# A two-layer decoder on one core: packed places on GpSimd, tiles' weights copied, four places and 2 KB pieces for the chosen experts

## What is computed

```
# layer 0: 32 experts (and two slices of a shared one), 4 per token, H = 128
scores = softmax(xf @ Wg); weights, indices = top_k(scores, 4)
for e in range(32):
    tok, w = tokens that chose e, their weights
    y = y.at[tok].add((silu(xf[tok] @ W1[e]) * (xf[tok] @ W3[e])) @ W2[e] * w)

# layer 1: 64 experts, 8 per token, 768 wide, at most 160 tokens for each expert
h = x_of_expert @ w1[e].T; x1, x2 = split(h)
out = (x1 * silu(x2)) @ w2[e].T          # weighted, and added to each token's row
```

## Time and profile before

| | us |
|---|---|
| median of 3 runs | 2603.03 (2599.43 to 2603.57) |
| the profiled execution | 2608.1 |
| its span | 2606.3 |
| packing rows | from about 383 to 580 |
| routed tiles | from 580 to 873 |
| chosen experts | from 1890 to 2606 |

### The profile page before, as it was taken

The page is one execution under the profiler, slowest core; times in us unless marked ns, Lnnn a source line. Parts: engine busy times, 40 slices in busy tenths (PEclk is TensorE's granted clock), DMA queues, the critical chain, the costliest instruction groups (busy, mean ns, idle before and its releaser), DMA issues. The chain is left out here.

```text
span 2606.3 us, 39064 instructions
## 1 busy us (share of the span) xinstructions
PE 2210.4 (85%) x11638; PEld 1487.9 (57%) x11639; DVE 1300.6 (50%) x2816; ACT 821.2 (32%) x1855; POOL 833.1 (32%) x1016
## 2 busy tenths in 40 slices
PE   6999759719999556888888887999999999999996
PEld 3445436507777322333343334656588888888885
DVE  5554246534444475776767673579133333333332
ACT  2222303204444224565555664311111111111111
POOL 2100016760000436444552110222324444444444
PEclk9999859859999778998999998999999999999998
DMA  9996117324555545433442112210067777777774
GB/s 323 372 369 221 45 43 271 116 102 146 156 158 156 150 100 114 93 69 87 102 111 81 48 34 84 106 32 16 29 213 253 253 252 252 250 248 248 250 253 134
DMA packets 254145, 412.86 MB, mean 158 GB/s; under 512 B 29960, under 2 KB 224113, under 8 KB 245852
## 3 DMA queue, kind: packets, MB, share of 16 engines
q1 hardware_dynamic: 215388, 351.92, 39.7%
q0 software_dynamic: 38656, 59.70, 10.5%
HBM read 262.05 MB, written 148.89 MB: 158 GB/s over the span
## 5 line engine op out<-in xcount | busy, mean ns | idle before, releaser
L2616 PE MATMUL me_hp<-me_xgT,me_w 128*128 128x160 f32 x3072 | 444.3, 303 | 27.0 <-DVE me_hid L2684 26.3
L2616 PEld LDWEIGHTS me_hp<-me_xgT,me_w 128*128 128x128 f32 x3072 | 421.7, 191 | 57.0 <-DVE me_hid L2684 33.5
L1371 DVE TENSOR_REDUCE hd_nmax<-hd_wide 128x2 f32<-128x1024 f32 x256 | 307.5, 1218 | 132.5 <-PE hd_wide L1116 131.8
L1300 ACT ACTIVATE hd_prob<-hd_slim 128x512 f32<-128x512 f32 x512 | 276.3, 602 | 193.5 <-PE hd_slim L1127 193.0
L2640 ACT ACTIVATE me_act_out<-me_hp 128x160 f32<-128x160 f32 x384 | 116.4, 303 | 591.2 <-PE me_hp L2616 545.4
L2684 DVE TENSOR_TENSOR me_hid<-me_act_out,me_hp 128x160 f32<-128x160 f32 x384 | 121.5, 320 | 316.9 <-ACT me_act_out L2640 311.4
L1127 PE MATMUL hd_slim<-hd_q_stack,hd_k_stack 100*128 100x512 bf16 x512 | 200.6, 395 | 43.8 <-ACT hd_prob L1300 31.9
L1116 PE MATMUL hd_wide<-hd_k_stack,hd_q_stack 97*128 97x512 bf16 x512 | 202.0, 399 | 30.6 <-DVE hd_rest L1365 15.8
L2529 POOL DMA_INDIRECT out_x<-me_oa,me_then_a x64 | 101.6, 1588 | 253.8 <-DMA out_x<-me_ob,me_then_b 241.0
L1999 PE MATMUL mr_e_hp<-mr_w,mr_e_xtT 128*128 x640 | 167.8, 385 | 0.8 <-issue 0.8
L2276 PE MATMUL me_r_hp<-me_r_xnT,me_r_sw 128*128 128x512 f32 x384 | 167.8, 593 | 0.0
(11 more groups left out here) (385 smaller groups left out, 3679.4 us busy)
## 6 DMA issues: line engine op xcount, KB each, us to landing
me_w<-in_L_ffn_w_exp SPq DMA_DIRECT2D x64, 1536.0 KB, 6.9
places<-z_zero SPq DMA_DIRECT2D x64, 1152.0 KB, 11.4
me_w_first<-in_L_ffn_w_exp SPq DMA_DIRECT2D x32, 768.0 KB, 8.9
me_w_second<-in_L_ffn_w_exp SPq DMA_DIRECT2D x32, 768.0 KB, 9.0
mr_e_xt<-places SPq DMA_DIRECT2D x160, 144.0 KB, 2.1
outputs<-mr_e_y SPq DMA_DIRECT2D x160, 128.0 KB, 1.7
part_rows<-hd_parts SPq DMA_DIRECT2D x48, 256.0 KB, 2.4
hd_k_stack<-part_rows SPq DMA_DIRECT2D x192, 64.0 KB
```

The costliest lines, as they stand in the source:

```text
L1300: nc.scalar.activation(prob[:, u, :], slim[:, slim_slot(bt, item), :], ACT.Exp, scale=D ** -0.5)\
L1371: nc.vector.tensor_reduce(nmax[:, g % 2, n // 2, c:c + 2], wide[:, at], AX.X, ALU.max, negate=True)\
L2616: last = nc.tensor.matmul(hp[:, f % 3, half * CAP:(half + 1) * CAP], w1[:, sl, c, cols], xgT[:, sl, c, :], start=(c == 0), stop=(c == DC - 1))
```

## The change

There are three parts.

First, `places_of_outputs` goes. VectorE only computes the shifts (`shifts`); GpSimd works out the rows in the block of the tiles, one bound at a time: 32 times a comparison with a product and an addition, on 128x128, with one operation ahead and a cast behind. Clearing the earlier semaphores now stands ahead of the weights' loads on SyncE.

Second, in the tiles VectorE copies a tile's first weights into one of four slots `w_now` with fixed addresses. TensorE takes these as the stationary side and the tokens as the moving one, so that the hidden tile comes out with its features on the partitions, ready for the second product. The transpose `hq` and the copy `hidT` go, and so does `expert_h`. TensorE reads one row of registers per turn, at the end of the turn before; VectorE reads eleven registers in one load.

Third, in the chosen experts `oa` gets four places instead of two, and the experts' weights lie in DRAM in pieces of 512 numbers (2 KB) per partition, which a DMA reads one by one where it read rows of 12 KB and 6 KB.

```diff
+                    earlier.clear(sp)
                     for n in range(0, E, 8):
...
-                    earlier.clear(sp)
                     sp.wait_ge(w_loaded, 16 * 2 * (E // 8))
...
-                        chain.link(nc.vector.tensor_tensor(reached[:], flat.unsqueeze(2).to_broadcast(wide),
-                                                           bounds[:].unsqueeze(1).to_broadcast(wide), ALU.is_ge))
-                        chain.link(nc.vector.tensor_tensor(reached[:], reached[:], shift_by[:].unsqueeze(1).to_broadcast(wide), ALU.mult))
-                        chain.link(nc.vector.tensor_reduce(moved[:], reached[:], AX.X, ALU.add))
-                        chain.link(nc.vector.tensor_tensor(moved[:], moved[:], flat, ALU.add))
-                        chain.link(nc.vector.tensor_copy(place_out[:].rearrange("p t n -> p (t n)"), moved[:]))
...
+                @block.gpsimd
+                def _(pool):
+                    chain = Chain(pool, shifted)
+                    flat = place_f[:].rearrange("p t n -> p (t n)")
+                    chain.link(nc.gpsimd.tensor_scalar(moved[:], flat, shift_by[:, 0:1], None, ALU.add))
+                    for e in range(1, E + 1):
+                        chain.link(nc.gpsimd.tensor_scalar(step[:], flat, float(CAP * e), shift_by[:, e:e + 1], ALU.is_ge, ALU.mult))
+                        chain.link(nc.gpsimd.tensor_tensor(moved[:], moved[:], step[:], ALU.add))
+                    chain.link(nc.gpsimd.tensor_copy(place_out[:].rearrange("p t n -> p (t n)"), moved[:]))
...
-                                for c in range(DC):
-                                    last = nc.tensor.matmul(hp[:, v, 0:2 * F], xtT[:, v, c, :],
-                                                            w1[:, bass.ds(e, 1), c, :].rearrange("p a n -> p (a n)"),
-                                                            start=(c == 0), stop=(c == DC - 1))
+                                for half in range(2):
+                                    for c in range(DC):
+                                        last = nc.tensor.matmul(hp[:, v, half * P:(half + 1) * P],
+                                                                w_now[:, (u - LAG_H) % W_SLOTS, c, half * F:(half + 1) * F],
+                                                                xtT[:, v, c, :], start=(c == 0), stop=(c == DC - 1))
...
-                                nc.tensor.transpose(hq[:, v, 0:P], hid[:, v, :], ident[:]).then_inc(hq_full, 1)
...
+                        if not last_ones:
+                            pe.load(regs_y, expert_y[0:1, bass.ds(i * UNROLL + UNROLL, UNROLL)])
...
-                                nc.scalar.activation(hidT[:, v, :], hq[:, v, 0:P], ACT.Copy).then_inc(hidT_ready, 1)
...
+                    def weights(reg, slot):
+
+                        e = dve.snap(reg, min_val=0, max_val=E - 1)
+                        nc.vector.tensor_copy(w_now[:, slot].rearrange("p c n -> p (c n)"),
+                                              w1[:, bass.ds(e, 1)].rearrange("p a c n -> p (a c n)")).then_inc(w_ready, 1)
...
+W_PIECE = 512
...
-            one = w_exp[bass.ds(e, 1)].rearrange("a p n -> p (a n)")
-            sp.dma_start(w1[:, place % 2].rearrange("p c n -> p (c n)"), one[:, 0:DC * 2 * F]).then_inc(w1_loaded[place % 2], 16)
-            sp.dma_start(w2_of.rearrange("p c n -> p (c n)"), one[:, DC * 2 * F:]).then_inc(w2_loaded[place], 16)
+            one = w_exp[bass.ds(e, 1)].rearrange("a c p n -> p (a c) n")
+            n1 = DC * 2 * F // W_PIECE
+            sp.dma_start(w1[:, place % 2].rearrange("p c n -> p (c n)").rearrange("p (c n) -> p c n", c=n1), one[:, 0:n1, :])\
+                .then_inc(w1_loaded[place % 2], 16)
+            sp.dma_start(w2_of.rearrange("p c n -> p (c n)").rearrange("p (c n) -> p c n", n=W_PIECE), one[:, n1:, :])\
+                .then_inc(w2_loaded[place], 16)
...
-        oa = k.sb("oa", [P, 2, D])
+        oa = k.sb("oa", [P, GATHERED, D])
...
-                pool.sem_inc(rows_free, 2)
+                pool.sem_inc(rows_free, GATHERED)
```

More of the change, by code:

```diff
@@ L1600, in mix_experts_routed @@
         w2 = k.sb("w2", [P, E, D])
+        place_f = k.sb("place_f", [P, NT, TOP])
+        bounds = k.sb("bounds", [P, E + 1])
+        shift = k.sb("shift", [P, E + 1])
+        shift_by = k.sb("shift_by", [P, E + 1])
         w_loaded = s.sem("w_loaded")
@@ L1980, in _ @@
                 def _(pe):
-                    regs_h = [pe.alloc_register(f"expert_h{u}") for u in range(UNROLL)]
                     regs_y = [pe.alloc_register(f"expert_y{u}") for u in range(UNROLL)]
                     def steps(i, first, last_ones):
-                        pe.load(regs_h, expert_h[0:1, bass.ds(i * UNROLL, UNROLL)])
-                        pe.load(regs_y, expert_y[0:1, bass.ds(i * UNROLL, UNROLL)])
                         for u in range(UNROLL):
@@ new lines, in steps @@
+                            if not (first and u < LAG_H) and not (last_ones and u > LAG_H - 1):
+                                v = (u - LAG_H) % 2
+                                pe.wait_ge(xt_ready, n)
+                                pe.wait_ge(w_ready, n)
+                                for half in range(2):
[3 more added lines that the diff above has]
+                                                                xtT[:, v, c, :], start=(c == 0), stop=(c == DC - 1))
+                                last.then_inc(hp_full, 1)
@@ L2044, in _ @@
                     dve.sem_inc(y_ready, 2)
-                    regs_y = [dve.alloc_register(f"weigh_y{u}") for u in range(UNROLL)]
+                    regs = [dve.alloc_register(f"expert{u}") for u in range(UNROLL + LAG_Y + AHEAD)]
+                    def weights(reg, slot):
+                        e = dve.snap(reg, min_val=0, max_val=E - 1)
+                        nc.vector.tensor_copy(w_now[:, slot].rearrange("p c n -> p (c n)"),
+                                              w1[:, bass.ds(e, 1)].rearrange("p a c n -> p (a c n)")).then_inc(w_ready, 1)
                     def steps(i, first, last_ones):
-                        dve.load(regs_y, expert_y[0:1, bass.ds(i * UNROLL, UNROLL)])
+                        now = regs[0:UNROLL] if last_ones else regs
+                        dve.load(now, expert_y[0:1, bass.ds(i * UNROLL, len(now))])
                         for u in range(UNROLL):
                             n = i * UNROLL + u
-                            if not (first and u < 1) and not (last_ones and u > 0):
-                                v = (u - 1) % 2
-                                dve.wait_ge(silu_done, n)
-                                nc.vector.tensor_tensor(hid[:, v, :], act_out[:, v, :], hp[:, v, F:2 * F], ALU.mult).then_inc(hid_ready, 1)
-                            if not (first and u < 3) and not (last_ones and u > 2):
+                            if not (first and u < LAG_Y) and not (last_ones and u > LAG_Y - 1):
                                 v = (u - LAG_Y) % UNROLL
@@ L2060, in steps @@
                                 dve.wait_ge(y_stored[v], i * 16 + (16 if u >= LAG_Y else 0))
-                                e = dve.snap(regs_y[u], min_val=0, max_val=E - 1)
+                                e = dve.snap(regs[u], min_val=0, max_val=E - 1)
                                 nc.vector.tensor_scalar(y[:, v, :], yp[:, v % 2, 0:D], xt[:, v, bass.ds(e + D, 1)], None, ALU.mult)\
                                     .then_inc(y_ready, 1)
+                            if not last_ones:
+                                weights(regs[u + LAG_Y + AHEAD], (u + AHEAD) % W_SLOTS)
+                            if not (first and u < LAG_H) and not (last_ones and u > LAG_H - 1):
+                                v = (u - LAG_H) % 2
+                                dve.wait_ge(silu_done, n)
+                                nc.vector.tensor_tensor(hid[:, v, :], act_out[:, v, :], hp[:, v, P:2 * P], ALU.mult).then_inc(hid_ready, 1)
+                    dve.load(regs[0:1], expert_y[0:1, LAG_Y:LAG_Y + 1])
+                    weights(regs[0], 0)
                     steps(0, True, False)
@@ L2549, in turn @@
                                 pool.sem_inc(rows_free, 1)
[L2550 removed]
+                            scatter(oa[:, m, :], then_a[:, m % 2, :])
                         else:
```

59 lines of the change are left out of this document (23 added, 36 removed).

## The result

The changed kernel takes 2590.14 us (median of 7 runs, 2589.03 to 2595.37) beside 2603.03 (7 runs): a ratio of 0.9952, 95% interval 0.994 to 0.9964. It is 13 us faster; I had forecast 63 us and a range that ends at 2572.

| us | before | after | change | forecast |
|---|---|---|---|---|
| start to first tile load | 580.35 | 574.22 | -6.1 | -6.6 |
| first tile load to the next block | 292.7 | 263.7 | -29.0 | -24 |
| next block to the first tails | 1039.7 | 1037.5 | -2.2 | 0 |
| first to last tails | 673.4 | 694.5 | **+21.1** | -33.8 |
| last tails to the end | 20.1 | 18.5 | -1.6 | -3 |

A forecast was written before the change was run, and what follows sets the result against it. Bounds: GpSimd's scatters in packing, TensorE in routed tiles, GpSimd's scatter-add landings in chosen experts. 6.6 + 13.4 + 10.6 + 33.8 + 3 = 67.4 us less, 4 given back: 2540 us from 2603.03, range 2522 to 2572.

The forecast's parts named there:

- Part one: Packing stage: without VectorE's two slow operations, GpSimd's two scatters of 4.25 and 4.29 us take 0.97; stage ends 6.6 us earlier.
- Part two, the tile: Routed tiles, bound by TensorE: a tile takes 1.545 us instead of 1.63, 160 times 0.084, 13.4 us less.
- Rival two: Routed tiles: VectorE sets the pace, its copy costing 0.691 us plus a wait; no gain there, 2564 us; chance 0.10.
- what I gave back for the tiles: Part of 4 us returned: GpSimd and VectorE meeting in the first 50 us, some 30 tiles by up to 0.07 us.
- Part two, the turn: Loop turns of routed tiles: one register row read instead of two saves half of 1.06 us, 20 times, 10.6 us; bounds 0 and 21.
- Part three: Chosen experts: GpSimd's chain falls from 21.72 to 20.63 us per pair, 33.8 us less, and 3 us less at the end.
- A row of 1 KB to be added that takes turns with such packets waits less than a quarter as long.: Chosen experts: smaller weight packets shorten scatter-add landings; 1.09 of 5.5 us contention per pair must go, for 33.8 us.
- Alone that moves no bound: Chosen experts: four places without smaller weight pieces leave GpSimd's chain at 21.72 us per pair; 3 us counted, at the stage's end.
- Bounds: nothing, and 37 us.: Chosen experts: the gain lies between nothing and 37 us, no more because TensorE's own work is unchanged.
- Rival one: Chosen experts: scatters land no sooner, GpSimd's chain stays at 21.72 us per pair, only 3 us gained; 2571 us; chance 0.17.
- Rival three: Chosen experts: weight loads in 2 KB pieces miss their expert; at 200 GB/s 60 us more, 2634 us; chance 0.05.
- The sign by which the prediction said it would fail most: Profile after, chosen experts: GpSimd still waits only for landings; the alternative sign was TensorE's waits in the tiles naming VectorE.

## Why the prediction was wrong, point by point

**Part one: right.** 6.1 us for 6.6, by the mechanism named: no scatter of the stage takes over 1.21 us. GpSimd's operations in the tiles' stage were 42 us busy (776 and 522 ns each) and ended at 622 us, 216 us before the end of the tiles that cover them.

**Part two, the tile: right.** 1.54 us for 1.545, 160 times 0.084. Rival two is refuted: the copies take 0.423 us. The Trainium skill ("SBUF — State Buffer", section "SBUF: two separate sides") has VectorE's two-port copies and GpSimd's operations shut each other out. The trace agrees in GpSimd's own times: its comparison takes 0.71 or 0.72 us in the 14 cases in which no copy overlaps it, and 0.79 to 1.02 in the 11 that a copy overlaps by 0.3 us or more. In VectorE's and TensorE's it shows next to nothing: GpSimd works from 574 to 622 us, and TensorE's tiles are 1.54 us apart from 584 us on, while VectorE's operations take 483 and 285 ns, as before. So what I gave back for the tiles (some 2 of the 4 us) wasn't due. The two slow operations of the earlier trace rows, which the prediction puts under the two-port rule, are no copies: they are TENSOR_TENSORs with two inputs in SBUF, which that section names beside the two-port mode, and only against a GpSimd operation that reads SBUF.

**Part two, the turn: the right sign, too small, and for the wrong reason.** I took half of 1.06 us because half of the loads go. Over eight tiles the turn costs 14.19 - 13.02 = 1.17 us before and 0.39 after, 15.6 us in all for 10.6. A second load at the turn's end costs nothing that shows, so what I had halved was not what the change saved; that it came near was luck. The Trainium skill ("DMA: Bandwidth & Descriptors", section "Latency and other measured facts") gives such a load a floor of about 600 ns; here a second load with products queued ahead of it has no visible price.

**Part three: wrong, +19.5 us for -36.8 (-33.8 and -3).** Three sentences failed.
- *"A row of 1 KB to be added that takes turns with such packets waits less than a quarter as long."* The packets became nearly as short (0.093 us, 0.27 of before), but the landings did not follow. Engines were 10% busier for the same bytes, and with two places the time from the tails' to the odd rows' scatter-add grew by 0.55 us. That contention with the loads is the cause was right (with the loads cut, TensorE is the bound). That shorter packets lessen it shows only where load and scatter-add start together, and there they take 0.66 us off a stretch of 10.55.
- *"Alone that moves no bound"*, on four places. Alone it costs 40 us (14 with 2 KB pieces). This is the step that failed most. GpSimd's wait only for landings was seen rightly, but I took a landing's time for a property of the transfer. It depended on when the next load began, and it was VectorE's wait for GpSimd, the 81.6 us of the earlier trace rows that the change removes, that fixed this. I read that wait as lag without cost.
- *"Bounds: nothing, and 37 us."* I excluded a loss, and the one reason given, that TensorE's work is unchanged, only bounds the gain. So the range ended at 2572 and the result at 2590. Parts one and two alone would be about 2603 less 37, 2566 us, inside it.

Rival one ("the scatters land no sooner") is nearest to what happened: the landings come no sooner, and its 2571 us lack the loss from the freed order. Rival three had a slower kernel in it, but by loads that miss their expert; here TensorE waits for gathers, not for weights. The sign by which the prediction said it would fail most came true: GpSimd still waits only for landings.

## What to carry to other kernels

A wait between two engines can hold transfers in a good order. Before a buffer is doubled to remove it, look at the offset between the transfers that share the DMA engines, in every period: if it is always the same, the wait may hold it, and the freed version may need a semaphore in its place. And where a chain of landings is the bound, fewer of them in a row helped more than smaller packets of the other transfers (two for three, with the gathers ahead: 20.55 us per pair, whatever the pieces).

## What the runs showed of the hardware

- A semaphore that GpSimd raises behind an indirect DMA is seen at the start of that 1.6 us instruction: the load that waited for it began within 0.1 us of it (41 of 46 pairs from 1960 to 2500 us in the two runs). Whoever wants it later has to put work between.
- The scatter-add that waits for another of 128 rows of 1 KB follows it after 9.1 to 11.4 us when a load of 2.3 MB begins between 2.6 us ahead of the first and 0.9 us behind. When the load begins 1.7 us behind or later, and the last one began at least 5.4 us ahead, it follows after 5.9 to 8.0 us, which GpSimd's own instructions take.
- Pieces of 2 KB hold the engines 10% longer for the same bytes than 8.2 KB packets (62.7% for 117.97 MB, 57.7% for 119.46).
- GpSimd takes 0.71 or 0.72 us for a comparison with a product on 128x128 while VectorE copies nothing, about as long as for an addition on twice the elements (0.735 us), and up to 1.02 us beside a VectorE copy from SBUF to SBUF.
